# A bias added by a one-row matmul in the second layer's bank instead of by GpSimd

## The reference, cut to what matters

```python
x = x + gnn(layernorm(x), adj)          # (8, 1024, 128), adj is (8, 1024, 1024)
x = x + experts(layernorm(x))

def gnn(x, adjacency):                  # H = 512
    agg = epsilon * x + einsum('bnm,bmd->bnd', adjacency, x)
    h = silu(rmsnorm(agg @ W1 + b1, rms_weight))
    return h @ W2 + b2
```

## Time and profile before

| | us |
|---|---|
| median of 3 runs | 699.27 (698.19 to 699.67) |
| the profiled execution: its own time | 698.98 |
| its span, first to last instruction | 697.2 |
| TensorE busy | 591.9 (85%) |
| VectorE busy | 453.2 (65%) |
| ScalarE busy | 359.3 (52%) |
| GpSimd busy | 385.1 (55%) |
| mean granted TensorE clock | 0.937 |

### The profile page before, as it was taken

One profiled execution on the slowest core, in us unless ns is written; L12 is line 12 of the kernel. 1 busy time (PEld: TensorE's weight loads), 2 busy tenths in 40 slices (PEclk: granted clock), 3 DMA queues, 4 the chain that ended last, 5 costly groups with the idle time before them and its releaser, 6 DMA issues.

```text
span 697.2 us, 13635 instructions
## 1 busy us (share of the span) xinstructions
PE 591.9 (85%) x4143; PEld 544.5 (78%) x4143; DVE 453.2 (65%) x1389; ACT 359.3 (52%) x852; POOL 385.1 (55%) x473
## 2 busy tenths in 40 slices
PE   1789899999989999999865499999999999999400
PEld 1668787878878787888754399999999999999400
DVE  2457989888898988888745345555454554555173
ACT  3257585866757586675542244444544445454200
POOL 4233268767676876767575236556555555556500
PEclk9889999999999999999995599999999999999855
DMA  7962344332444432245412655556555555563099
GB/s 262 324 184 116 121 153 148 124 111 80 147 152 153 149 114 111 90 146 153 153 39 79 205 206 191 197 183 216 181 195 195 172 204 189 185 206 126 3 398 323
DMA packets 59760, 116.49 MB, mean 167 GB/s; under 512 B 8399, under 2 KB 35072, under 8 KB 59688
## 3 DMA queue, kind: packets, MB, share of 16 engines
q1 hardware_dynamic: 50792, 98.62, 41.8%
q0 software_dynamic: 8896, 17.00, 7.2%
HBM read 61.80 MB, written 25.63 MB: 125 GB/s over the span
## 4 chain that ended last, share of the span: by engine, by line
PE 64%; DVE 12%; ACT 9%; issue 5%; DMA 4%; POOL 3%; SPq 1%; POOLq 0%; DVEq 0%; ACTq 0%
PE ps_y L628 10%; PE ps_g L628 9%; PE ps_agg L462 6%; PE ps_agg L464 5%; PE ps_agg L463 5%; PE ps_t L469 5%; PE ps_y L576 4%; PE ps_h L462 4%; PE ps_h L463 4%; PE ps_h L464 4%; DVE adjT_lo L943 3%; ACT adjT_hi L664 3%; DMA adj_in<-parts 3%; DVE hn L1026 3%; PE ps_t L605 2%
## 5 line engine op out<-in xcount | busy, mean ns | idle before, releaser
L902 POOL DMA_INDIRECT parts<-adj_in,goes x150 | 145.7, 971 | 125.7 <-ACT adj_in L781 60.1
L852 POOL DMA_INDIRECT slots<-rows,dest x128 | 128.5, 1004 | 43.5 <-issue 38.3
L781 ACT ACTIVATE adj_in<-adj_in,share 128x128 f32<-128x128 f32 x150 | 49.4, 392 | 134.8 <-issue 123.0
L943 DVE TENSOR_TENSOR adjT_lo<-ps_t,adjT_hi 128x512 fp32r<-128x512 f32 x128 | 88.1, 689 | 34.0 <-ACT adjT_hi L664 31.0
L664 ACT ACTIVATE adjT_hi<-ps_t 128x512 fp32r<-128x512 f32 x128 | 76.1, 596 | 63.5 <-PE ps_t L469 63.3
L469 PE MATMUL ps_t<-ident,adj_in 128*128 128x128 f32 x512 | 79.8, 281 | 13.2 <-POOL adj_in L838 13.2
L469 PEld LDWEIGHTS ps_t<-ident,adj_in 128*128 128x128 f32 x512 | 66.5, 146 | 31.1 <-issue 14.4
L462 PE MATMUL ps_agg<-adjT_hi,xn_hi 128*128 128x512 f32 (+1 forms) x152 | 69.9, 460 | 10.5 <-DVE adjT_lo L943 10.5
L1128 DVE CAST goes<-adj_in 128x3 int32<-128x3 f32 x50 | 9.6, 192 | 103.7 <-DMA parts<-adj_in,goes 94.3
L628 PE MATMUL ps_g<-W2e,hn 128*128 x600 | 71.0, 275 | 0.0
L628 PE MATMUL ps_y<-W2e,hb 128*128 x600 | 71.0, 275 | 0.0
(11 more groups left out here) (176 smaller groups left out, 1317.8 us busy)
## 6 DMA issues: line engine op xcount, KB each, us to landing
adj_in<-in_adj SPq DMA_DIRECT2D x16, 2048.0 KB, 10.0
W1cur<-W1e SPq DMA_DIRECT2D x26, 512.0 KB, 3.1
adj_in<-slots SPq DMA_DIRECT2D x50, 196.5 KB, 2.5
xn_hi<-W1e SPq DMA_DIRECT2D x12, 512.0 KB, 3.1
xn_lo<-W1e SPq DMA_DIRECT2D x12, 512.0 KB, 3.1
W1e<-parts SPq DMA_DIRECT2D x4, 1024.0 KB, 8.2
adj_in<-parts SPq DMA_DIRECT2D x4, 1024.0 KB, 16.0
out<-x_all SPq DMA_DIRECT2D x8, 512.0 KB, 6.2
```

The source lines that it names most:

```text
L781: ins = act.activation(ye[ku][:, j, :], yb[ku % 2][:, j, :], ACT.Copy, scale=share[ku][:, j:j + 1])
L852: pool.indirect_dma_start(out=slots, out_offset=bass.IndirectOffsetOnAxis(ap=dest[1 - par][:, c, j:j + 1], axis=0), in_=rows[1 - par][:, c ...
L902: pool.indirect_dma_start(out=parts, out_offset=bass.IndirectOffsetOnAxis(ap=goes[ku][:, j:j + 1], axis=0), in_=ye[ku][:, j, :], in_offset ...
L943: dve.tensor_tensor(adjT_lo[m % 2][:, :], ps_t[m % 2][:, :], adjT_hi[m % 2][:, :].bitcast(FP32), ALU.subtract).then_inc(s_lo, 1)
```

## The change

b2 no longer goes to x on GpSimd. Instead TensorE begins each second layer with one matmul of a row of ones (1 x 128) with b2 (1 x 128, read four times in a row), which fills all 512 columns of the bank with b2; the 16 matmuls of the layer accumulate on it, so that none of them starts the bank. The function `x_plus_b2`, its semaphore, its waits on GpSimd and VectorE's wait for it are gone. A memset of the row of ones is new.

```diff
+        one_row = sb("one_row", [1, P])
...
-        s_xb = sem("x_plus_b2_ready")
...
                     wait(pe, s_x1, q)
                     for c in range(HC):
                         pe.wait_ge(s_silu, 4 * q + c + 1)
+                        if c == 0:
+                            pe.matmul(ps_y[:, :].rearrange("p (t d) -> p t d", d=D), one_row[:, :],
+                                      b2s[0:1, None, :].broadcast_to([1, GT, D]), start=True, stop=False)
                         for j in range(GT):
                             ins = pe.matmul(ps_y[:, j * P:(j + 1) * P], siluT[:, c, j * P:(j + 1) * P],
-                                            W2s[:, c, :], start=(c == 0 and j == 0),
-                                            stop=(c == HC - 1 and j == GT - 1))
+                                            W2s[:, c, :], start=False, stop=(c == HC - 1 and j == GT - 1))
                     ins.then_inc(s_y, 1)
...
+            pool.memset(one_row[:, :], 1.0)
...
-            def x_plus_b2(b):
-                xv = x_all[:, bass.ds(b * TPB, TPB), :] if not isinstance(b, int) else x_all[:, b * TPB:(b + 1) * TPB, :]
-                pool.tensor_tensor(xv, xv, b2s[:, None, :].broadcast_to([P, TPB, D]), ALU.add).then_inc(s_xb, 1)
...
-                if isinstance(g, int) and g == 0:
-                    pool.wait_ge(s_const, 16 * 9)
-                if par == 0 and has(g, 0):
-                    pool.wait_ge(s_xn, b * 2 + 2)
-                    pool.sem_inc(s_turn, 1)
-                    x_plus_b2(b)
...
                     dve.wait_ge(s_y, q + 1)
-                    dve.wait_ge(s_xb, b + par)
```

## The result

The changed kernel is slower: 702.74 us, median of 5 runs, against 698.19 for the kernel before on the same chip; ratio 1.0073, 95% interval 1.0046 to 1.01. On another chip, 700.13 us (10 runs) against 697.03, ratio 1.0048 (1.0028 to 1.0067). The forecast was 697.1, the range 694.3 to 700.8.

The account below looks back on a forecast made before the run. TensorE was taken to bound the first part (busy 76.69 of 81 us). 698.98 - 4.9 (start) + 2.7 (middle) = 696.8; with the runs' median 0.3 above the profiled execution, the forecast was 697.1, range 694.3 to 700.8.

Parts of the forecast that it names:

- The stalls of VectorE: GpSimd's addition delays VectorE's hn scaling (six TensorE waits, 8.2 us) and W1_lo in step 0 (2.1 us); both stalls go.
- The added matmul: One-row f32 matmul before each second layer: 0.92 us, bounds 0.23 to 1.84; full in even steps, 0.64 in odd.
- the dear case: Rival: reading one partition or repeated b2 makes the one-row matmul cost 1.84 us, +12.9, so 710; chance 0.07.
- two matmuls that cost nothing: The b2 matmuls of steps 15 and 16, forecast hidden behind the wait for expert weights and GpSimd's scatters.
- Start -4.9: Step 0: 2.1 us from W1_lo's stall going, 2.8 from the clock staying up; bounds -2.1 and about -5.5.
- The step's own bound: Start gains at most about 5.5 us: group 2's adjacency, issued at 35.5, lands up to 9.7 us later.
- The clock, for which I took 2.8 us: Start: the last three products of step 0 run at 2.4 GHz instead of 1.2, 2.8 us less.
- The rival that the clock falls at 28.5 us anyway: Rival: the clock falls despite the shorter idle time; start -2.1 instead of -4.9, so 699.9; chance 0.25.
- Middle +2.7: Middle of the first part: matmuls 6.44 in even and 4.48 in odd steps, less 8.2 of removed waits.
- Step 16 "hidden": The matmul of step 16 costs nothing, as GpSimd computes the factors only at 366.81, behind its scatters.
- The expert part unchanged: The expert part behind 400 us contains neither the addition nor the added matmul and keeps its length.

Follow-up runs that it names:

- addition gone: Changed kernel without its one-row matmul, so b2 is left out of the second layer; 684.99 us against 697.03 for the kernel before, ratio 0.9822.
- the second of the forms: Changed kernel with the b2 matmul last in even steps, and in odd steps reading b2 stored four times over; one run, 701.18 us, beside 697.03.
- addition moved: Kernel before with GpSimd's additions moved to the end of step 0 and of odd steps 1 to 13, no matmul; 688.37 us against 696.89, ratio 0.9874.

## Why the prediction was wrong

- **The stalls of VectorE: right in the middle, taken for certain at the start.** The two instructions took 0.88 and 0.69 us, and the waits for hn went. The forecast was 8.2 us; steps 1 to 15 gave 9.6, some 0.2 a step more than the waits themselves, and where that comes from wasn't traced. The stall in step 0, however, was read from one trace, in which GpSimd was ahead by 0.05 us; in both traces of the matmul alone, which keeps the addition, VectorE was ahead and there was no stall.
- **The added matmul: mis-sized.** Its step said 4 x 0.23 = 0.92 us, from the layer's own matmuls. It is 1.05, and 1.07 with the layer behind it; why it is dearer than four inside the layer stays open. Steps 1 to 14 cost 13.2 us, where 10.9 were forecast, and the whole run 15.1. The point from which the dear case decides was put at 1.2 us, on a gain of 13.1 and on two matmuls that cost nothing; with 12.0 gained and 15.1 paid at 1.07, the change would be even at about 0.85, if what is paid goes with the price (an estimate).
- **"Start -4.9": wrong, -3.1.** The step's own bound named the cause and then sized it wrongly: the landing of group 2 was taken at up to 9.7 us. The five issues of the earlier trace rows begin with it, but the profile of before gives no landing for that one, so the 9.7 belongs to a later issue. In the changed kernel it took 12.2, and in the other five traces of chips at 697 us that show it, one of them with the addition in its old place, 12.5 to 13.3. The clock, for which I took 2.8 us, was worth nothing beyond that, as the traces in which it stayed up show. The rival that the clock falls at 28.5 us anyway was wrong too: it survived 0.80 us of idle time, fell behind 2.17, and neither mattered.
- **Middle +2.7: +3.6.** Both terms were too small, by 2.3 and 1.4 us. That the sum is only 0.9 off is luck.
- **Step 16 "hidden": all but 0.6 us.** That step took its cover from the kernel before, at its clock. The clock was at 0.50 from 350.6 to 364.3 us instead of 356.2 to 359.6, and the cover was short by 0.56 us.
- **The expert part unchanged: wrong by 1.8 us, cause open.** One of its 50 tiles (at 602 to 604 us, in the matmul alone at 621) takes 6.7 to 7.2 us instead of 5.1 in all four traces with a one-row f32 matmul on chips at 697 us (two of the changed kernel, the matmul alone, the second of the forms), and in none of the three without (before, addition gone, addition moved). There VectorE comes to the first instruction of a tile late, here in the changed kernel:

```profile
606.10 0.17 DVE L1120 CAST goes<-adj_in 128x3 int32<-128x3 f32 x1 [5.08 <-PE ps_t L607]
```

In the kernel before the same instruction ran at 603.02 after 2.15 us of idle time. In these seven traces it goes with the matmul, but nothing here shows that the matmul is the cause.

The sum: -3.1 + 3.6 + 0.4 + 1.8 = +2.7 of the +2.8 us between the two profiled executions. The medians give +3.1 and +4.5. From the forecast's -2.2 to +2.7 it is 4.9 us: 1.8 at the start (the landing of group 2), 0.9 in the middle (matmuls 2.3 dearer, less 1.4 of unforeseen gain), 0.4 up to the expert part and 1.8 inside it, whose cause is open. The steps that failed are thus the price of the one-row matmul and the landing that caps the start, and the expert part was taken as unchanged without a reason beyond its having neither operation.

## What to carry to other kernels

Before work moves from an idle engine to the one that bounds the kernel, ask whether it can stay where it is and stand elsewhere in the order: the cost was that a SBUF-to-SBUF addition on GpSimd stood in front of a VectorE scaling, and moving it gave 8.5 us, where giving it to TensorE lost 3.1 to 4.5. A bias by matmul costs TensorE its columns whatever its rows, 1.07 us per 512 f32 columns here. Where a term of a sum ends at a transfer, look up the landing of that very transfer, and if the profile has none, say so and widen the bound. And where two engines start within 0.1 us of each other, look in more than one trace before you count on who is held up.

## What the hardware showed that I had not expected

- The clock fell behind waits of 1.5 us for 3.4 us at a time in the kernel with both matmul and addition, and never between 60 and 350 us in the kernel before, whose waits there are 1.3 to 1.5 us long. A wait on the bounding engine can so cost 1.7 us more than it lasts (five times, some 9 us).
- Of a GpSimd addition and a VectorE instruction that collide, the one that starts first keeps its time: 0.72 us for VectorE's subtraction when it was 0.12 us ahead (the addition 2.83), 2.85 us when it was 0.05 us behind (the addition 2.35).
- Two one-row fp32r matmuls of 512 columns advance TensorE by 0.66 us, one f32 one by 1.05.
- The same kernel takes 697 us on some chips and 784 to 803 on others, with pauses inside a row of matmuls whose operands are all there; the pauses lie beside large transfers, and of a gain of 1.8% only 0.6 or 0.2% is seen there.
